# A spectral cross-attention and expert kernel: every projection from high and low parts, row sums folded twice, logits in four column groups, and a new order of the work

## The chip, the cores and the metric

The kernel runs on one core of a Trainium2 chip. The engines that matter here are TensorE (PE in the profile: matrix products; PEld is its loading of the stationary operand), VectorE (DVE), ScalarE (ACT), GpSimd (POOL) and SyncE (SP, which only issues DMAs). They run side by side and wait for each other through semaphores. The metric is the device time of one execution in microseconds (us), lower is better. The profile is of one execution of its own.

## The reference

`x` and `ctx` are 32 sequences of 512 rows of 512 numbers. Cut to what matters:

```
x = x + attention(layernorm(x), ctx)
x = x + ffn(layernorm(x))
attention: q = rows of x, scaled by a logistic map of their norm and by position
           Q, K, V = q @ Wq.T + bq, mem @ Wk.T + bk, mem @ Wv.T + bv   (mem = ctx * constant)
           QKV = hamilton(hamilton(fft(Q)*f, fft(K)*f), fft(V)*f)      (fft along the 512 rows)
           return real(ifft(QKV))
ffn:       logits = layernorm(tokens) @ gate.T; top-1 of 8 experts, capacity 4096
           out = tokens + softmax weight * (gelu(token @ wi[e]) @ wo[e])
```

## The kernel before

There are two stages. The first takes the sequences one after the other and ends with each token's row written to the slot of its expert. The second runs the eight experts over the slots. The change touches only the first.

In the first stage the Fourier transform is taken before the projection, since both are linear, and only 256 of the 512 frequencies are computed, because the signal is real. One sequence goes through these steps:

- SP loads `x_in` and `c_in`. ACT and POOL compute row statistics (`sums_x`, `squares_x`, `stats1`, the map in `logistic`, `scales1`), and ACT scales the rows in `q_of`.
- DVE folds the 512 rows to 256 sums for the even frequencies and 256 differences for the odd ones (`folds_q`, `folds_c`, two operations of 128x1024 each).
- `dft(b, w, u)` on PE: for the context (w = 0) and the query (w = 1), and for each of four blocks u of 128 columns, four f32 products with 256 moving columns against a constant matrix of cosines and sines, two for each half of a 512-column bank, `xt_ps[u % 2]`. ACT copies the bank to `c_spec` or `q_spec`.
- K and V are projected from a high and a low part of the spectrum. Both are of the type fp32r, which PE takes in one pass and rounds; high times high, low times high and high times low are added up. ACT makes `c_high` and DVE makes `c_low` (`context_low`). Q is projected by f32 products (`project(b, k, s)`; k counts Q, K and V for even and odd frequencies and s is the real or the imaginary half).
- DVE turns the spectra into complex pairs (`convert`), multiplies the quaternions (`products`, `sums`, `back_to_parts`). `inverse` on PE transforms back, and DVE adds the residual (`add_even`, `add_odd`).
- `turn` transposes the rows into `xt_ps`, `token_block` copies them to `x_tok_t`, and `logits` multiplies them by the gate: for each of four row tiles four f32 products of 8 moving columns. `choose` and `place` on DVE pick the expert and the slot. `sums_x2`, `squares_x2`, `stats2` and `base_of` compute the second layernorm's numbers and the residual row, and `store` writes it to HBM. `scatter` writes the row to its slot.

Each engine runs one hand-written list, `body(b)`, in which every call names how many sequences it lags, such as `project(b - 1, 2, 0)`. The engines take their lists strictly in order. Nothing else sets the order but the semaphores. PE's `xt_ps` has two banks, used in turn by `dft` and `turn`; `pair` has two, used in turn by the projections k, and freed by `convert`; `even_ps` and `odd_ps` serve the inverse transform, the logits and the ranks.

Of the kernel before, what the change touches and what calls it, by code (L numbers as in the profile page):

```python
# [22 lines left out]
P = 128  # L23
# [30 lines left out]
def forward_matrix():  # L54

    n = np.arange(256)[:, None]
    j = np.arange(128)[None, :]
    m = np.empty((256, 2, 2, 128))
    for tile in (0, 1):
        angle = 2 * np.pi * (((2 * j + tile) * n) % 512) / 512  # L60
        m[:, tile, 0], m[:, tile, 1] = np.cos(angle), -np.sin(angle)
    m[:, 0, 1, 0] = 1 - 2 * (np.arange(256) % 2)
    return m.reshape(2, 128, 2, 256).transpose(1, 0, 2, 3).reshape(128, -1).astype(np.float32)


def inverse_matrix():
# [6 lines left out]
    for tile in (0, 1):  # L73
        f = (2 * np.arange(128) + tile)[:, None]
        e = h[f] * np.exp(2j * np.pi * ((f * n) % 512) / 512) / 512
        m[:, tile, 0], m[:, tile, 1] = e.real, -e.imag
# [50 lines left out]
def xattn_moe_kernel(nc, x, ctx_in, wq, wk, wv, bq, bk, bv, gate, gamma, beta, wi, wo, out):  # L127
# [4 lines left out]
    c_fwd = nc.inline_tensor(forward_matrix(), "c_fwd").ap()  # L132
# [3 lines left out]
    c_tri = nc.inline_tensor(np.triu(np.ones((P, P), np.float32), 1), "c_tri").ap()  # L136
    c_eye = nc.inline_tensor(np.eye(P, dtype=np.float32), "c_eye").ap()
# [8 lines left out]
    with outer:  # L146
# [11 lines left out]
        with ExitStack() as mem:  # L158
# [6 lines left out]
            fwd = sb("fwd", [P, 2, 2, 256])  # L165
            inv = sb("inv", [P, 2, 2, 256])
            w_q = sb("w_q", [P, CB, DIM])

            w_kh, w_kl, w_vh, w_vl = (sb(n, [P, CB, DIM], f32r) for n in ("w_kh", "w_kl", "w_vh", "w_vl"))
            c_high, c_low = (sb(n, [P, CB, 512], f32r) for n in ("c_high", "c_low"))  # L170
# [7 lines left out]
            gate_g = sb("gate_g", [P, CB, EXPERTS])  # L178
# [13 lines left out]
            q_spec, c_spec = (sb(n, [P, CB, 512]) for n in ("q_spec", "c_spec"))  # L192
# [15 lines left out]
            real_row = sb("real_row", [1, 3, 2, DIM])  # L208
# [7 lines left out]
            x_tok_t = [sb(f"x_tok_t{i}", [P, CB, P]) for i in (0, 1)]  # L216
# [22 lines left out]
            SETUP_DMAS = 15  # L239
            ZEROED = len(values) + 5  # L240
# [6 lines left out]
            w_split, c_split = sem("w_split"), sem("c_split")  # L247
# [12 lines left out]
            f1_mm, f1_ev = sem("f1_mm"), sem("f1_ev")  # L260
# [5 lines left out]
            g_mm, g_ev, logit_mm = sem("g_mm"), sem("g_ev"), sem("logit_mm")  # L266
            route, exp_done, rank_mm = sem("route"), sem("exp_done"), sem("rank_mm")
# [6 lines left out]
            SETUP = 14  # L274

# [11 lines left out]
            with nc.Block() as block:  # L287

                @block.sync
                def _(sp):  # L290
# [9 lines left out]
                    def load_x(b):  # L300
                        if not on(b) or isinstance(b, int) and b < 2:
                            return
                        sp.wait_ge(qf_ready, b * 2)
                        sp.dma_start(x_in, seq(x, b)).then_inc(x_loaded, 16)

                    def load_c(b):
                        if not on(b) or isinstance(b, int) and b < 2:
                            return
                        sp.wait_ge(cf_ready, b * 2)
                        sp.dma_start(c_in, seq(ctx_in, b)).then_inc(c_loaded, 16)  # L310

                    def real_out(b):
# [3 lines left out]
                        sp.dma_start(bins_in, real_row[:].rearrange("o a s n -> o (a s n)")).then_inc(real_left, 16)  # L316
                        if last_sequence(b):
                            sp.wait_ge(qf_ready, BATCH * 2)
                            sp.wait_ge(cf_ready, BATCH * 2)
# [62 lines left out]
                    sp.dma_start(fwd[:].rearrange("p a b c -> p (a b c)"), c_fwd).then_inc(fwd_in, 16)  # L382
                    sp.dma_start(pos[:], c_pos).then_inc(pos_in, 16)
                    for dst, src in ((signs[:].rearrange("p a b c -> p (a b c)"), c_sgn),
                                     (tri32, c_tri), (eye[:], c_eye), (token[:], c_tok),
                                     (iota8[:].rearrange("p t e -> p (t e)"), c_exp),
                                     (w_q[:], wq.rearrange("(k p) n -> p k n", p=P)),
                                     (kv_raw[:, 0], wk.rearrange("(k p) n -> p k n", p=P)),
                                     (kv_raw[:, 1], wv.rearrange("(k p) n -> p k n", p=P)),
                                     (inv[:].rearrange("p a b c -> p (a b c)"), c_inv),  # L390
                                     (gate_t[:], gate.rearrange("(k p) e -> p k e", p=P)),
# [6 lines left out]
                    sp.wait_ge(cf_ready, 2)  # L398
                    sp.dma_start(c_in, seq(ctx_in, 1)).then_inc(c_loaded, 16)
                    sp.wait_ge(qf_ready, 2)  # L400
# [4 lines left out]
                    def body(b):  # L405
                        real_spread(b - 3)
                        real_gather(b - 3)
                        real_store(b - 3)
                        store(b - 4)
# [15 lines left out]
                def _(pe):  # L425
                    def dft(b, w, u):
# [6 lines left out]
                        if u == 0:  # L433
                            pe.wait_ge(ready, b * 2 + 2)
# [1060 lines left out]
```

## Time and profile before

| | |
|---|---|
| median of 3 runs | 3565.24 us (3561.56 to 3566.55) |
| the profiled execution | 3560.93 us, span on the core 3559.1 us |
| mean granted TensorE clock | 0.986 of full speed |
| PE busy | 3459.5 us (97%) |
| DVE busy | 2547.8 us (72%) |
| ACT busy | 1610.9 us (45%) |
| POOL busy | 1264.8 us (36%) |

The span is measured from the first instruction to the last. The busy shares are over both stages; the windows of the trace part them. In a line of the timeline, the first number is the start, the second how long the group took; the ends of products are modelled and overlap the next, so that the time of a product is read from one start to the next. An f32 product leaves two records, an fp32r product one.

### The profile page before, as it was taken

What the parts mean: (1) busy time and instruction counts of PE and PEld (TensorE: products, weight loads), DVE (VectorE), ACT (ScalarE), POOL (GpSimd) and SP (SyncE); (2) the same over time, 40 slices, a digit from 0 to 9 for tenths busy, and PEclk for the clock granted to TensorE, in tenths of its full rate; (3) what the DMA queues carried; (4) which work ended last, traced back from release to release, by engine and by line L of the source; (5) the groups of instructions that cost most, each with busy time, mean ns of one, the idle gap of its engine ahead of it and who ended that gap; (6) DMA issues with size and microseconds to landing.
All of it is one profiled execution on the core that took longest, in us unless ns stands there. A gap on an engine that the chain in (4) does not pass through costs nothing. (4 is left out here: it accounts for less than half of the span.)

```text
span 3559.1 us, 46918 instructions
## 1 busy us (share of the span) xinstructions
PE 3459.5 (97%) x15056; PEld 2634.4 (74%) x15056; DVE 2547.8 (72%) x3536; ACT 1610.9 (45%) x2948; POOL 1264.8 (36%) x1607
## 2 busy tenths in 40 slices
PE   7999999999999999999999959999999999999998
PEld 5766777767776777776777648888888888888886
DVE  4999999999999999989899954444444444444443
ACT  4545545455454554545545333333333333333332
POOL 2556656466565565656566530000000000000000
PEclk9999999999999999999999969999999999999999
DMA  5421221211212112121121123333333333333331
GB/s 201 153 104 59 73 83 59 81 62 59 83 48 95 60 59 95 71 83 48 59 95 60 60 81 104 109 119 118 120 119 119 117 119 106 107 105 119 107 108 41
DMA packets 223433, 326.65 MB, mean 92 GB/s; under 512 B 36880, under 2 KB 102672, under 8 KB 223280
## 3 DMA queue, kind: packets, MB, share of 16 engines
q1 hardware_dynamic: 207952, 307.97, 25.1%
q0 software_dynamic: 15360, 16.99, 1.4%
q8 instruction: 86, 1.41, 0.2%
q14 instruction: 35, 0.29, 0.0%
HBM read 256.82 MB, written 101.97 MB: 101 GB/s over the span
## 5 line engine op out<-in xcount | busy, mean ns | idle before, releaser
L1372 ACT ACTIVATE act<-hid_ps 128x512 f32<-128x512 f32 x256 | 153.1, 598 | 797.5 <-PE hid_ps L1299 797.5
L1433 DVE CAST act_h<-act 128x512 fp32r<-128x512 f32 x256 | 109.3, 427 | 523.2 <-ACT act L1372 523.2
L1253 POOL TENSOR_TENSOR tally<-tally,unit 1x1 f32<-1x1 f32 x16 | 2.9, 180 | 1350.2 <-DVE mixed L1445 1350.2
L468 PE MATMUL pair<-w_q,q_spec 128*128 128x512 f32 x1024 | 457.6, 595 | 11.6 <-DVE s L989 10.7
L1299 PE MATMUL hid_ps<-tok_h,w_h 128*128 128x512 f32 x1024 | 405.5, 396 | 0.2 <-issue 0.2
L1299 PE MATMUL hid_ps<-tok_l,w_h 128*128 128x512 f32 x1024 | 399.3, 390 | 0.0
L1299 PE MATMUL hid_ps<-tok_h,w_l 128*128 128x512 f32 x1024 | 398.7, 389 | 0.0
L1315 PE MATMUL out_ps<-w_l,act_h 128*128 128x512 f32 x1024 | 398.5, 389 | 0.0
L1314 PE MATMUL out_ps<-w_h,act_l 128*128 128x512 f32 x1024 | 398.3, 389 | 0.0
L1313 PE MATMUL out_ps<-w_h,act_h 128*128 128x512 f32 x1024 | 398.3, 389 | 0.0
L1427 DVE TENSOR_TENSOR w_l<-w_raw,w_h 128x2048 fp32r<-128x2048 f32 x128 | 293.4, 2293 | 90.9 <-ACT w_h L1366 90.9
L468 PEld LDWEIGHTS pair<-w_q,q_spec 128*128 128x128 f32 x1024 | 191.9, 190 | 220.9 <-issue 204.7
L667 ACT ACTIVATE q_spec<-xt_ps 128x512 f32<-128x512 f32 x128 | 76.5, 598 | 534.8 <-PE xt_ps L442 534.8
L442 PE MATMUL xt_ps<-fwd,c_fold 128*128 128x256 f32 x1024 | 253.4, 392 | 15.7 <-DVE c_fold L921 11.6
L1366 ACT ACTIVATE w_h<-w_raw 128x2048 fp32r<-128x2048 f32 x128 | 244.5, 1911 | 10.0 <-PEq L287 10.0
L442 PEld LDWEIGHTS xt_ps<-fwd,c_fold 128*128 128x128 f32 x1024 | 198.8, 197 | 60.1 <-issue 27.1
L442 PEld LDWEIGHTS xt_ps<-fwd,q_fold 128*128 128x128 f32 x1024 | 195.7, 191 | 55.7 <-issue 28.7
L442 PE MATMUL xt_ps<-fwd,q_fold 128*128 128x256 f32 x1024 | 232.9, 381 | 2.8 <-DVE q_fold L921 2.8
L1299 PEld LDWEIGHTS hid_ps<-tok_l,w_h 128*128 128x128 f32 x1024 | 192.3, 188 | 41.1
L1299 PEld LDWEIGHTS hid_ps<-tok_h,w_h 128*128 128x128 f32 x1024 | 192.6, 188 | 39.4 <-issue 1.6
L1314 PEld LDWEIGHTS out_ps<-w_h,act_l 128*128 128x128 f32 x1024 | 192.2, 188 | 40.0
L1313 PEld LDWEIGHTS out_ps<-w_h,act_h 128*128 128x128 f32 x1024 | 192.2, 188 | 39.9
(172 smaller groups left out, 7931.5 us busy)
## 6 DMA issues: line engine op xcount, KB each, us to landing
w_raw<-in_L_ffn_wi SPq DMA_DIRECT2D x128, 512.0 KB, 3.5
w_raw<-in_L_ffn_wo SPq DMA_DIRECT2D x128, 512.0 KB, 4.5
w_raw<-in_x SPq DMA_DIRECT2D x32, 1024.0 KB, 5.4
w_raw<-in_ctx SPq DMA_DIRECT2D x32, 1024.0 KB, 7.7
x_res<-in_x SPq DMA_DIRECT2D x31, 1024.0 KB, 9.8
out<-x_res SPq DMA_DIRECT2D x31, 1024.0 KB, 4.3
slots<-rows SPq DMA_DIRECT2D x4, 4160.0 KB, 17.3
got<-slots SPq DMA_DIRECT2D x15, 1040.0 KB, 7.6
```

Of the source, the lines that this page charges most:

```text
L442: last = nc.tensor.matmul(ps[:, eo * 256:eo * 256 + 256], folded[:, eo, t, u * P:(u + 1) * P], fwd[:, t, eo, :], start=(t == 0), stop=(t = ...
L468: last = nc.tensor.matmul(pair[k % 2][:, s, :], spec[:, c, tile * 256 + s * P:tile * 256 + (s + 1) * P], w[:, c, :], start=(c == 0 and n = ...
L667: nc.scalar.activation((c_spec, q_spec)[w][:, u, :], xt_ps[u % 2][:], ACT.Copy).then_inc(f1_ev, 1)
L1253: nc.gpsimd.tensor_tensor(tally[:], tally[:], unit[:], ALU.add).then_inc(tallied, 1)
L1299: last = nc.tensor.matmul(hid_ps[i % 2][:], a[:, c, :], b[:, c, :], start=first_, stop=last_)
L1313: nc.tensor.matmul(out_ps[t][:], ah, oh, start=(i == 0), stop=False)
L1314: nc.tensor.matmul(out_ps[t][:], al, oh, start=False, stop=False)
L1315: last = nc.tensor.matmul(out_ps[t][:], ah, ol, start=False, stop=(i == ISTEPS - 1))
L1366: nc.scalar.activation(w_h[k % RING][:], w_raw[k % 2][:], ACT.Copy).then_inc(wh_ready, 1)
L1372: nc.scalar.activation(act32[i % 2][:], hid_ps[i % 2][:], ACT.Gelu).then_inc(gelu, 1)
L1427: v.tensor_tensor(w_l[k % RING][:], w_raw[k % 2][:], w_h[k % RING][:].bitcast(f32), ALU.subtract).then_inc(wl_ready, 1)
L1433: v.tensor_copy(act_h[i % 4][:], act32[i % 2][:]).then_inc(ah_ready, 1)
```

## The change

The change has five parts, all in the first stage.

1. **Query from parts too.** `w_q` becomes `w_qh` and `w_ql`, and the query's spectrum `q_high` and `q_low`. All six projections of a sequence are then three fp32r products for each block, where Q had one f32 product.
2. **Low parts made in the bank.** ACT copies the bank of a transformed block rounded to `c_high` or `q_high` (`spectrum_high`), PE adds minus the identity times that high part to the same bank (`remove_high`, one fp32r product with 512 moving columns), and ACT copies what is left (`spectrum_low`). DVE's `context_low` and ACT's `context_high` are gone, and so are `c_spec` and `q_spec`.
3. **Rows folded twice.** The even frequencies are split once more: the 256 sums are folded again into 128 sums and 128 differences (`fold_again`), so that each half of the even frequencies takes one product of 128 moving columns.
4. **Logits in four column groups.** `gate_w` is now the stationary operand with 32 columns, and the tokens move. Each of the four blocks of the contraction writes its own 32 partitions of `even_ps`, ACT copies these partial sums (`logits_out`), and `logits_turn` adds and transposes them by four products with a constant matrix.
5. **New order** on every engine's list. Two small changes go with it: `real_row` uses three partitions, and the constant DMAs of the setup are 16 instead of 15.

The diff, cut to its core:

```diff
-                            pe.wait_ge(ready, b * 2 + 2)
+                            pe.wait_ge(ready, b * FOLD + FOLD)
...
-                        for eo in range(2):
-                            for t in range(2):
-                                last = nc.tensor.matmul(ps[:, eo * 256:eo * 256 + 256],
-                                                        folded[:, eo, t, u * P:(u + 1) * P], fwd[:, t, eo, :],
-                                                        start=(t == 0), stop=(t == 1))
+                        even = ps[:, 0:256].rearrange("p (s h j) -> p h s j", s=2, h=2)
+                        for h in range(2):
+                            nc.tensor.matmul(even[:, h], folded[:, 0, h, u * P:(u + 1) * P], fwd_e[:, h],
+                                             start=(h == 0), stop=True,
+                                            skip_group_check=True)
+                        for t in range(2):
+                            last = nc.tensor.matmul(ps[:, 256:512], folded[:, 1, t, u * P:(u + 1) * P], fwd_o[:, t],
+                                                    start=False, stop=True,
+                                            skip_group_check=True)
                         last.then_inc(f1_mm, 1)
+
+                    def remove_high(b, w, u):
...
+                        pe.wait_ge(f1_high, b * 8 + w * 4 + u + 1)
+                        nc.tensor.matmul(xt_ps[u % 2][:], minus_eye[:], (c_high, q_high)[w][:, u, :],
+                                         start=False, stop=True, skip_group_check=True).then_inc(f1_rest, 1)
...
-                        terms = ((q_spec, w_q),) if which == 0 else ((c_high, wh), (c_low, wh), (c_high, wl))
+                        high, low = (q_high, q_low) if which == 0 else (c_high, c_low)
+                        terms = ((high, wh), (low, wh), (high, wl))
...
-                            last = nc.tensor.matmul(even_ps[:, t * EXPERTS:(t + 1) * EXPERTS], x_tok_t[t % 2][:, c, :],
-                                                    gate_g[:, c, :], start=(c == 0), stop=(c == CB - 1))
+                            last = nc.tensor.matmul(even_ps[32 * c:32 * c + 32, h * 256:h * 256 + 256], gate_w[:, c, :],
+                                                    x_tok_t[:, :, c, :], start=True, stop=True, tile_position=(0, 32 * c))
...
+                        pe.wait_ge(logit_ev, b + 1)
+                        for t in range(ROWT):
+                            o = LOGITS + t * EXPERTS
+                            last = nc.tensor.matmul(odd_ps[:, o:o + EXPERTS], parts[:, t * P:(t + 1) * P], chosen[:],
+                                                    start=True, stop=True)
...
+                        nc.scalar.activation((c_high, q_high)[w][:, u, :], xt_ps[u % 2][:], ACT.Copy).then_inc(f1_high, 1)
...
+                        act.wait_ge(f1_rest, b * 8 + w * 4 + u + 1)
+                        nc.scalar.activation((c_low, q_low)[w][:, u, :], xt_ps[u % 2][:], ACT.Copy).then_inc(f1_low, 1)
...
-                        for eo, op in ((0, ALU.add), (1, ALU.subtract)):
-                            v.tensor_tensor(dst[:, eo], src[:, 0:2], src[:, 2:4], op).then_inc(ready, 1)
+                        v.tensor_tensor(dst[:, 1], src[:, 0:2], src[:, 2:4], ALU.subtract).then_inc(ready, 1)
+                        v.tensor_tensor(src[:, 0:2], src[:, 0:2], src[:, 2:4], ALU.add).then_inc(ready, 1)
+
+                    def fold_again(b, src, dst, ready):
+                        dve.wait_ge(ready, b * FOLD + 2)
+                        v.tensor_tensor(dst[:, 0, 0], src[:, 0], src[:, 1], ALU.add).then_inc(ready, 1)
+                        v.tensor_tensor(dst[:, 0, 1], src[:, 0], src[:, 1], ALU.subtract).then_inc(ready, 1)
```

PE's new list, in which one place matters below (`dft` and `remove_high` share the two banks):

```diff
+                        project(b - 2, 5, 1)
+                        dft(b - 1, 0, 1)
+                        remove_high(b - 1, 0, 0)
+                        remove_high(b - 1, 0, 1)
+                        dft(b - 1, 0, 2)
+                        dft(b - 1, 0, 3)
+                        remove_high(b - 1, 0, 2)
...
+                        logits(b - 3, 1)
                         project(b - 1, 4, 0)
+                        logits_turn(b - 3)
+                        dft(b, 0, 0)
                         project(b - 1, 4, 1)
+                        project(b - 1, 5, 0)
```

On PE, where the query's blocks are transformed between the two inverse transforms, this stood before (L442 is `dft`, L502 `inverse`; the rows named ISA or REGISTER_ALU carry waits):

```order
L442 MATMUL xt_ps<-fwd,q_fold 128x256 x4
L124 REGISTER_ALU
L442 MATMUL xt_ps<-fwd,q_fold 128x256 x4
L124 REGISTER_ALU
L442 MATMUL xt_ps<-fwd,q_fold 128x256 x4
L499 ISA
L502 MATMUL even_ps<-r_spec,inv 128x512 x2
```

And this stands on PE behind a body's start now, for the context's blocks 1 to 3 (L468 and L472 are `dft`, L483 is `remove_high`; the banks alternate):

```order
L468 MATMUL xt_ps<-fwd_e,c_fold 128x2x64 x2
L472 MATMUL xt_ps<-fwd_o,c_fold 128x256 x2
L482 ISA
L483 MATMUL xt_ps<-c_high,minus_eye 128x512
L482 REGISTER_ALU
L483 MATMUL xt_ps<-c_high,minus_eye 128x512
L468 MATMUL xt_ps<-fwd_e,c_fold 128x2x64 x2
L472 MATMUL xt_ps<-fwd_o,c_fold 128x256 x2
```

Four products have become two short ones and two long ones, and each block has a product of its own between the two copies by ACT. The second `remove_high` stands directly behind the first.

On ACT, this stood before around the residual pass (L698 is `base_of`, L667 `spectrum`, L683 `real_part`, L691 `real_bin`, L637 `decay`, L643 and L647 `logistic`, ten steps in all; the scaling of the query's rows, `q_of`, comes further down):

```order
L691 ACTIVATE real_row<-pair0 1x1024
L707 ACTIVATE x_tok_t1<-xt_ps1 128x512
L698 ACTIVATE x_res<-rows0 128x512 x4
L667 ACTIVATE c_spec<-xt_ps0 128x512
L683 ACTIVATE re1<-pair1 128x512
L691 ACTIVATE real_row<-pair1 1x1024
L637 ACTIVATE map_e<-norm1 128x4
L643 ACTIVATE map_y0<-map_s,minus_half 128x4
L647 ACTIVATE map_y1<-map_y0,centre 128x4
```

And this stands there now (L757 is `base_of`, L712 `q_of`, L727 `spectrum_high`, L733 `spectrum_low`, L742 `real_part`, L782 `exps`):

```order
L757 ACTIVATE x_res<-rows1 128x512 x4
L710 REGISTER_ALU
L712 ACTIVATE w_raw0<-w_raw0,q_bias,q_scale 128x512 x4
L138 REGISTER_ALU
L727 ACTIVATE c_high<-xt_ps0 128x512
L740 REGISTER_ALU
L138 REGISTER_ALU
L742 ACTIVATE re0<-pair0 128x512
L727 ACTIVATE c_high<-xt_ps1 128x512
L733 ACTIVATE c_low<-xt_ps0 128x512
L781 ISA
L782 ACTIVATE e_over<-over 128x32
```

The map has moved ahead of `base_of`, `q_of` stands directly behind it, and the first copies of the context's spectrum, for which `remove_high` and the next `dft` wait, stand behind both.

## Rows read from the trace of the kernel before

**Rows 1.** The page: busy time, share of the span and instructions.

```profile
PE 3459.5 (97%) x15056; PEld 2634.4 (74%) x15056; DVE 2547.8 (72%) x3536; ACT 1610.9 (45%) x2948; POOL 1264.8 (36%) x1607
```

**Rows 2.** Busy time in three stretches: loops, drain, experts.

```profile
core 0: us, PE busy (x) PEld busy (x) DVE busy (x) ACT busy (x) POOL busy (x), PEclk, DMA share, GB/s
1000.00:1500.00 500.00, 494.92 (x2127) 353.15 (x2126) 454.05 (x665) 267.57 (x589) 287.63 (x372) 1.00 0.21 74
2055.00:2111.00 56.00, 27.19 (x120) 18.89 (x120) 26.69 (x60) 18.72 (x43) 24.12 (x36) 0.59 0.17 57
2111.00:3559.00 1448.00, 1427.61 (x6400) 1179.72 (x6400) 690.84 (x832) 525.97 (x577) 67.78 (x82) 0.99 0.32 110
```

**Rows 3.** PE timeline, one body: start us, us, line, operation, count.

```profile
1000.98 0.48 PE L468 MATMUL pair<-w_vh,c_high 128*128 128x512 f32 x1
1001.29 0.40 PE L468 MATMUL pair<-w_vh,c_low 128*128 128x512 f32 x1
...
1006.52 1.89 PE L442 MATMUL xt_ps<-fwd,c_fold 128*128 128x256 f32 x8
1008.25 3.60 PE L468 MATMUL pair<-w_q,q_spec 128*128 128x512 f32 x8
...
1044.35 7.13 PE L468 MATMUL pair<-w_q,q_spec 128*128 128x512 f32 x16
1051.32 0.95 PE L527 MATMUL even_ps<-gate_g,x_tok_t 128*128 128x8 f32 x8
1052.13 0.63 PE L516 MATMUL xt_ps<-eye,rows 128*128 128x128 f32 x4
1052.60 1.91 PE L527 MATMUL even_ps<-gate_g,x_tok_t 128*128 128x8 f32 x16
```

**Rows 4.** PE timeline, fifteen bodies later: the same projection.

```profile
1994.75 7.11 PE L468 MATMUL pair<-w_q,q_spec 128*128 128x512 f32 x16 [0.56 <-DVE s L989]
```

**Rows 5.** DVE groups, 500 to 2000 us: count, busy us, mean ns, idle before.

```profile
L986 DVE TENSOR_TENSOR s<-re,pair 128x256 f32<-128x256 f32 x141 | 57.9, 411 | 13.5 <-ACT real_row L691 13.5
...
L921 DVE TENSOR_TENSOR q_fold<-w_raw 128x1024 f32<-128x1024 f32 x48 | 56.5, 1217 | 23.1 <-ACT w_raw L655 23.1
L937 DVE TENSOR_TENSOR c_low<-c_spec,c_high 128x2048 fp32r<-128x2048 f32 x24 | 54.7, 2279 | 0.0
...
L1062 DVE TENSOR_TENSOR rows<-x_res,even_ps 128x512 f32<-128x512 f32 x48 | 32.7, 682 | 40.1 <-DMA x_res<-in_x 36.0 <-PE even_ps L502 4.1
...
L1086 DVE TENSOR_TENSOR logit<-even_ps,rows 128x32 f32<-128x32 f32 x23 | 4.4, 192 | 32.7 <-PE even_ps L527 32.7
```

**Rows 6.** DVE timeline, three operations of one group of sums.

```profile
1007.48 1.22 DVE L1026 TENSOR_TENSOR prod<-prod 128x1024 f32<-128x1024 f32 x1
1008.73 0.69 DVE L1028 TENSOR_TENSOR s<-prod 128x512 f32<-128x512 f32 x1
1009.34 0.68 DVE L1029 TENSOR_TENSOR s<-prod 128x512 f32<-128x512 f32 x1
```

**Rows 7.** POOL timeline: first row of the query's scale, first and last of the second statistics.

```profile
1009.81 0.27 POOL L808 TENSOR_TENSOR st<-map_y,slope 128x4 f32<-128x4 f32 x1 [3.38 <-ACT map_y L647]
...
1048.71 2.31 POOL L825 TENSOR_TENSOR tt<-square,inv_dim 128x4 f32<-128x4 f32 x1 [4.50 <-ACT unused L606]
...
1061.63 2.25 POOL L835 TENSOR_TENSOR rows<-neg,rows 128x4 f32<-128x4 f32 x1
```

**Rows 8.** ACT timeline: copies, and the two passes that wait for POOL.

```profile
1013.84 2.93 ACT L655 ACTIVATE w_raw<-w_raw,q_bias,q_scale 128x512 f32<-128x512 f32 x4 [1.66 <-POOL q_bias L812]
...
1028.35 0.60 ACT L667 ACTIVATE q_spec<-xt_ps 128x512 f32<-128x512 f32 x1 [10.62 <-PE xt_ps L442]
...
1043.90 1.91 ACT L676 ACTIVATE c_high<-c_spec 128x2048 fp32r<-128x2048 f32 x1
...
1063.92 2.93 ACT L698 ACTIVATE x_res<-rows 128x512 f32<-128x512 f32 x4 [6.33 <-POOL rows L835]
```

**Rows 9.** PE timeline at the start.

```profile
53.84 0.80 PE L468 MATMUL pair<-w_kh,c_high 128*128 128x512 f32 x1 [3.96 <-DVE w_vl L944]
```

More of the change, by code:

```diff
@@ L274, in xattn_moe_kernel @@
             SETUP = 14
+            FOLD = 4
+            LOGITS = 64
             TILE_DONE = (3, 7, 4, 8)
@@ L549, in body @@
+                        inverse(b - 3, 1, 0)
+                        inverse(b - 3, 1, 1)
+                        turn(b - 3, 1 - p, 0)
+                        project(b - 1, 0, 0)
+                        project(b - 1, 0, 1)
+                        turn(b - 3, 1 - p, 1)
                         project(b - 1, 1, 0)
                         project(b - 1, 1, 1)
-                        dft(b, 0, 1)
-                        logits(b - 3, 3)
+                        turn(b - 3, 1 - p, 2)
+                        logits(b - 3, 0)
@@ L573, in body @@
-                        turn(b - 2, p, 1)
-                        project(b, 0, 0)
-                        project(b, 0, 1)
-                        logits(b - 2, 0)
-                        turn(b - 2, p, 2)
-                    for b in range(6):
+                        project(b - 1, 5, 0)
+                    for b in range(7):
                         body(b, b % 2)
-                    with pe.Fori(6, 30, 2) as b:
-                        body(b, 0)
-                        body(b + 1, 1)
@@ L583, in _ @@
-                    for b in range(30, BATCH + 3):
+                    with pe.Fori(7, 29, 2) as b:
+                        body(b, 1)
+                        body(b + 1, 0)
+                    for b in range(29, BATCH + 4):
                         body(b, b % 2)
@@ L749, in _ @@
+                        logits_out(b - 3)
+                        base_of(b - 3, 1 - p)
+                        q_of(b)
+                        spectrum_high(b, 0, 0)
+                        real_part(b - 1, 4)
+                        spectrum_high(b, 0, 1)
+                        spectrum_low(b, 0, 0)
+                        exps(b - 3)
+                        spectrum_low(b, 0, 1)
+                        spectrum_high(b, 0, 2)
+                    for b in range(6):
                         body(b, b % 2)
-                    with act.Fori(7, 29, 2) as b:
-                        body(b, 1)
-                        body(b + 1, 0)
@@ L753, in _ @@
-                    for b in range(29, BATCH + 4):
+                    with act.Fori(6, 30, 2) as b:
+                        body(b, 0)
+                        body(b + 1, 1)
+                    for b in range(30, BATCH + 3):
                         body(b, b % 2)
```

328 lines of the change are left out of this document (175 added, 153 removed).

## The prediction

> **What bounds the kernel now.** I read the page first: PE is busy for 97% of the span and DVE for 72% [rows 1]. These are means over two stages, and the windows part them. In the loops PE is busy for 494.9 of 500 us and DVE for 454.1; in the experts' 1448 us DVE is under one half, and the change does not touch them [rows 2]. So the change acts in the first stage, and there PE sets the pace, with DVE close behind. The timeline gives the period: the query's first projection starts at 1044.35 and, fifteen bodies later, at 1994.75, so 950.4 / 15 = 63.36 us a sequence [rows 3, 4]. PE's busy part of it is 0.990 x 63.36 = 62.7 us, and 0.6 us is waits.
>
> For DVE, the groups tell what it waits for. In the 1500 us, or 23.7 bodies, it sat idle 13.5 us for ACT's one-row copy, 23.1 for the scaled query rows, 36.0 for the residual's load and 32.7 for the logits [rows 5]: 105.3 / 23.7 = 4.4 us a body. The rest of its idle time lies inside its own chains. DVE's own work thus takes 63.4 - 4.4 = 59.0 us. This is the second floor, and only 3.7 us under PE's.
>
> **The change on PE, per sequence.** Starts are compared with starts, since the ends of products are modelled.
>
> - Query from parts. Sixteen f32 records, which are eight products of 512 columns, take 1051.32 - 1044.35 = 6.97 us. The 24 fp32r products of a V projection take 1006.52 - 1000.98 = 5.54 us for the same amount of work, so 0.23 us each [rows 3]. Two query projections: 2 x (6.97 - 5.54) = 2.9 us less.
> - Folded twice. A block's four f32 products of 256 columns take 1008.25 - 1006.52 = 1.73 us, so 0.43 us each [rows 3], as much per column as those of 512. Two of the four halve their columns. No row shows an f32 product of 128 columns. By columns it is 0.215 us. From below the loading of the weights bounds it: four products with 8 columns take 1052.13 - 1051.32 = 0.81 us, 0.20 each [rows 3], and that lies under 0.215. From above it is 0.43, no gain. I take 0.215, since it is next to the row for 8 columns, where only the loading counts: 8 x 2 x 0.215 = 3.4 us less (bounds 0 and 3.7).
> - Removing the high part. Eight fp32r products of 512 columns are added. In a row each takes 0.23 us, but the first behind an f32 product takes 1001.29 - 1000.98 = 0.31 [rows 3]: 8 x 0.31 = 2.5 us more (bounds 1.8 and 2.5).
> - Logits. The four row tiles cost 4 x 0.81 = 3.2 us. `logits_turn` is four products of 8 columns again, 0.8 us. The eight products with 256 moving columns and 32 stationary ones are not in the trace. If the four column groups run side by side, two sets cost about as much as two products of 256 columns, 2 x 0.43, with some 0.1 us each for starting, 1.1 us. If they don't, they are two sets of four such products, 2 x 1.73 = 3.5 us [rows 3]. I take the first, since the groups share neither columns nor output partitions: 3.2 - 0.8 - 1.1 = 1.3 us less (other bound: 1.1 us more).
>
> About this, "TensorEngine Tiling (Array Packing)" of the Trainium skill (Performance Considerations and Key Properties) says that four column groups bring up to four times the speed, and that a change of tiling drains the engine. "TensorE: Matmul & The Clock Gate" (Part 3) gives 2.38 times for three column groups; with that factor a set would take 1.73 / 2.38 = 0.73 us (an estimate from that page), and the sum would be 0.4 us a sequence higher. The same part says that weight loads run ahead of products in flight only where row groups differ, which here they don't; by that the groups would follow each other, which is the rival below. No row here shows column groups.
>
> Sum on PE: 62.7 - 2.9 - 3.4 + 2.5 - 1.3 = 57.6 us.
>
> **The change on DVE.** `context_low` goes: 54.7 us for 24 [rows 5], 2.2 us each by starts. Two folds get two operations of 512 columns each, which start 1009.34 - 1008.73 = 0.61 us apart, and each must see the operation before it finished, as in the sums, where the next starts 1008.73 - 1007.48 = 1.25 us after an operation of 1.22 [rows 6], some 0.1 us later than without. That is 4 x 0.61 + 2 x 0.1 = 2.6 us. DVE's floor rises by 0.4 us to 59.4 us and stands above PE's sum. What PE gives up beyond that is worth nothing.
>
> **The waits that the change adds.** ACT gets eight more copies from the bank at 0.60 us [rows 8], `logits_out` at 0.60, and loses `context_high`, 1.91 [rows 8]: 3.5 us more on an engine that is busy for 267.6 of 500 us [rows 2]. That costs nothing as work. It costs as latency, for PE now waits for ACT twice for each block. At most places another product lies between. At two it doesn't. Behind `dft(0, 1)` stand two `remove_high` and then `dft(0, 2)`, which needs ACT to have copied block 1's high part and block 0's low part: 2 x 0.60 and about 0.3 us of hand-over (an estimate), less the 0.5 us of the two products: 1.0 us. The last `remove_high` of the query waits for block 3's copy, 0.6 us. Both together 1.6 us, with everything else on PE queued behind.
>
> The same two copies stand on ACT behind `base_of` and `q_of`, which wait for POOL. There the second statistics take from 1048.71 to 1063.9, 15.2 us, and `base_of` waited 6.33 us for them [rows 7, 8]. In the new order `squares_x2` follows projection 1 on ACT. From there PE has listed, until it needs the bank for that `dft(0, 2)`, projections 2 to 5 (22.2 us), two transposes (0.9), both sets of logits and their turn (1.9), two blocks (2.6) and one `remove_high`: 28 us. The other engines have two copies, the small `decay` and the squares, some 5 us (an estimate), 15.2 for the statistics, 1013.84 - 1009.81 = 4.0 for the query's scale [rows 7, 8], 2.9 for its rows [rows 8] and 2 for the copies: 29 us. So this chain ties with PE's own work, and costs 0 to 2 us. I add 0.4.
>
> Period: 57.6 + 0.6 (the waits of now) + 1.6 + 0.4 = 60.2 us. That is 0.8 above DVE's floor of 59.4, so DVE lets it through, but only if most of its 4.4 us of waits go. They should, as three of the four end when PE or ACT behind PE delivers, and DVE now is the later one.
>
> **The sum.** The first stage has 31 periods between its first and last sequence: 31 x (63.36 - 60.2) = 98 us less. At the start K's first projection stood at 53.84, behind the low part of V's weights [rows 9]; the weights now come in the same way with one split more (2.2 us), and the folds are 0.7 us longer: 3 us more. The drain, 56 us of it with PE half idle [rows 2], goes through the same chain; I put it at nothing, give or take 10 us. The profiled execution took 3560.9 us, the median 3565.2. So 3560.9 - 98 + 3 = 3466, and 2 us more for the middle between the two: **3468 us**.
>
> **The rivals.**
>
> - *The column groups follow one another* (14%). 2.4 us a sequence dearer on PE: 62.6 us, 31 x 0.76 = 24 less, 3541 us. For it: the weights are f32 and every f32 product loads twice. Against: nothing in the rows.
> - *DVE's floor is all that counts* (13%). If PE's waits at the banks vanish behind DVE's pace: 59.4 us, 31 x 3.96 = 123 less, 3442 us.
> - *ACT and POOL pace it* (12%). If the chain above costs its 2 us, or `remove_high` waits at more places: 61.8 us, 31 x 1.56 = 48 less, 3518 us.
> - *Slower: DVE keeps its waits* (7%). DVE's floor has gone up by 0.4 us. If its 4.4 us of waits stay, because each hangs on a chain through POOL and DMA and not on PE's pace (the load of the residual alone is 36.0 us of them [rows 5], and it starts when `base_of`'s rows are stored), the period is 59.4 + 4.4 = 63.8 us, 31 x 0.4 = 14 us more with 3 for the start: 3580 us. It decides from waits of 4.0 us on.
>
> My forecast has 50%, with a range of its own from 3445 to 3500. The other 4% are a net of nothing. The range over all reaches from 3432 to 3542, which leaves out the slower case and the ends. What a measurement of this kernel can tell from no change is about 0.2%, 7 us. Faster by more than that: 88%; within it: 5%; slower: 7%.
>
> **What would show it.** Right: two Q projections starting some 60 us apart; a block's transform of 1.3 us; each set of logits 0.4 to 0.6 us; PE's share in the loops down to 96% with waits for ACT's copies before L483 and L468; DVE's share up to 96%. Wrong if f32 products of 128 columns cost as much as 256 (3.4 us a sequence back, 100 us in all), if the copies by ACT delay every block, or if DVE's groups show its waits for the residual or the query as large as before.

## The result and the profile after

The changed kernel takes **3429.7 us** (median of 4 runs, 3429.1 to 3429.9) against 3563.4 us for the kernel before in the same comparison (4 runs): a ratio of 0.9625, with a 95% interval of 0.9608 to 0.9642. That is 134 us less. The forecast of 3468 us was 97 us under the 3565 us of the kernel before, and the result lies 2.3 us below the low end of the range of 3432 to 3542. The sign and the order of size were right; the period was 1 us too long.

The page after has a span of 3427.8 us and this busy line, which answers to [rows 1]:

```profile
PE 3286.5 (96%) x15568; PEld 2597.8 (76%) x15568; DVE 2571.6 (75%) x3633; ACT 1736.4 (51%) x3206; POOL 1422.2 (41%) x1608
```

The windows, which answer to [rows 2]; the experts begin 132 us earlier now, so their stretch is taken there, and the drain is left out:

```profile
core 0: us, PE busy (x) PEld busy (x) DVE busy (x) ACT busy (x) POOL busy (x), PEclk, DMA share, GB/s
1000.00:1500.00 500.00, 485.84 (x2427) 372.13 (x2426) 493.21 (x740) 315.01 (x686) 369.41 (x404) 1.00 0.24 79
...
1979.00:3427.00 1448.00, 1427.42 (x6400) 1179.18 (x6400) 690.80 (x832) 526.00 (x577) 68.35 (x82) 0.99 0.33 110
```

The experts are the same 1427.4 us of PE in the same 1448 us, so everything happened in the first stage. There the two engines have changed places. DVE went from 454 to 493 of 500 us, and PE from 495 to 486. PE's share of the whole span, still 96%, hides this. DVE's 75% hides it more: it is a mean over loops at 98.6% and experts at 48%.

The period is read from an operation that comes once a sequence, the copy `logits_out` on ACT. The columns are count, shortest/median/longest ns, first and last start:

```profile
L776 ACT ACTIVATE x_tok_t<-even_ps x16: 597/598/601, 1004.1 to 1892.5; 128x512 f32<-128x512 f32 x16
```

So (1892.5 - 1004.1) / 15 = **59.23 us** a sequence, against 63.36 before. 31 times the difference is 128 us of the 134. DVE's list alone was put at 59.4.

Some of these 128 us are TensorE's clock, which the forecast did not look at. (PEclk in the windows is the granted clock as a share of full speed.) The kernel before in one stretch of its loops (columns as above):

```profile
611.00:613.00 2.00, 2.00 (x7) 1.55 (x6) 1.97 (x3) 1.85 (x4) 1.92 (x2) 0.50 0.00 0
```

Here the granted clock was 0.50, the lower of TensorE's two levels (1.2 GHz), with PE busy throughout. Short stretches like it lie near 228, 928, 1119 and 1689 us too. Read from one copy `c_high` to the next, the sequences from 400 to 1900 us in which one of them fell took 64.3 to 64.5 us, and the others 62.9 to 63.7. In the changed kernel the clock stayed full from 40 us to the drain (1.00 in the window above). At some 1.2 us each the five make about 6 us of the 128 (an estimate from these periods), and two of them, 0.2 us a sequence, are in the 63.36.

What each engine waited for, 500 to 1900 us, which is 23.6 sequences. First PE, with total us, times and the longest; then DVE:

```profile
PE pair L506 <- DVE s L1067: 18.4, 23, 0.8
PE xt_ps L483 <- ACT q_high L727: 11.0, 24, 0.5
PE xt_ps L483 <- ACT c_high L727: 10.4, 23, 0.5
DVE rows L1140 <- PE even_ps L540: 1.3, 1, 1.3
```

Of DVE's waits before, 105 us for the one-row copy, the query's rows, the residual and the logits [rows 5], not one is left. The rows of those two engines also give PE's account: 0.9717 x 59.23 = 57.6 us busy, 21.4 / 23.6 = 0.9 us for ACT's copies, 18.4 / 23.6 = 0.8 us for DVE. The last is the sign that DVE leads: PE finds the `pair` bank not yet read by `convert`.

DVE's groups, 500 to 2000 us, answer to [rows 5]. They are `convert`, the query's fold, and the context's fold, which is the same operation:

```profile
L1064 DVE TENSOR_TENSOR s<-re,pair 128x256 f32<-128x256 f32 x144 | 58.9, 409 | 0.0
L996 DVE TENSOR_TENSOR q_fold<-w_raw 128x1024 f32<-128x1024 f32 x23 | 32.1, 1397 | 0.0
L996 DVE TENSOR_TENSOR c_fold<-w_raw 128x1024 f32<-128x1024 f32 x23 | 28.0, 1217 | 0.0
```

The first two showed 13.5 and 23.1 us of waiting before, and the sum that takes the residual 36.0 for its load; for these causes they now show none. The query's fold takes 1397 ns, though it took 1217 before [rows 5] and the context's still does. What runs beside it is GpSimd's work on the one-row copy:

```profile
1017.77 1.58 POOL L925 TENSOR_TENSOR real_in<-real_in,bias 16x96 f32<-16x96 f32 x1
1019.04 1.41 DVE L996 TENSOR_TENSOR q_fold<-w_raw 128x1024 f32<-128x1024 f32 x1
```

In the two bodies looked at (1000 to 1119 us), two of the eight operations of 128x1024 in `sums` stand beside later GpSimd operations on the same row and take 1.60 and 1.47 us; the other six take 1.21. With the rest of the query's folds (1335 ns for 1217, 802 for 683) that is 0.2 + 0.1 + 0.1 + 0.4 + 0.3 = about 1.1 us a sequence by which DVE's list is longer beside GpSimd. In the kernel before, the same sums were 0.4 us longer than at 1.21 each (means of 1.25 and 1.28) and the folds not at all.

The terms on PE, from its timeline (start us, us, line, operation, count). First a set of logits in column groups, then a stretch of the new transforms:

```profile
1003.38 0.64 PE L565 MATMUL even_ps<-x_tok_t,gate_w 128*32 128x256 f32 x8
1003.95 0.50 PE L506 MATMUL pair<-w_kh,c_high 128*128 128x512 f32 x1
...
1018.33 0.58 PE L483 MATMUL xt_ps<-c_high,minus_eye 128*128 128x512 f32 x1
1019.37 0.50 PE L483 MATMUL xt_ps<-c_high,minus_eye 128*128 128x512 f32 x1 [0.45 <-ACT c_high L727]
1019.86 0.71 PE L468 MATMUL xt_ps<-fwd_e,c_fold 128*128 128x128 f32 x4
...
1025.22 0.61 PE L468 MATMUL xt_ps<-fwd_e,q_fold 128*128 128x128 f32 x4
1025.66 1.03 PE L472 MATMUL xt_ps<-fwd_o,q_fold 128*128 128x256 f32 x4
1026.53 0.61 PE L468 MATMUL xt_ps<-fwd_e,q_fold 128*128 128x128 f32 x4
```

A set of logits (8 records, four f32 products with 256 columns) takes 1003.95 - 1003.38 = 0.57 us, where four ordinary products of 256 columns took 1.73 [rows 3]: the four groups run side by side. A block's transform takes 1026.53 - 1025.22 = 1.31 us, of which the two products with 128 columns take 0.44. Both were forecast (0.55 and 1.3). The wait in brackets is at the first of the two places where the prediction saw PE held by ACT, behind `dft(0, 1)`; the prediction gave that place 1.0 us.

### The profile page after: what moved, and what is told of

It reads as the page before. It is cut to its first block and busy times, and to the rows that moved or that the text cites. A ratio compares the mean times of both kernels' runs of the same rounds, so it can differ in the third digit from the quotient of the medians.

```text
span 3427.8 us, 48342 instructions
## 1 busy us (share of the span) xinstructions
PE 3286.5 (96%) x15568; PEld 2597.8 (76%) x15568; DVE 2571.6 (75%) x3633; ACT 1736.4 (51%) x3206; POOL 1422.2 (41%) x1608
## 5 line engine op out<-in xcount | busy, mean ns | idle before, releaser
L742 ACT ACTIVATE re<-pair 128x512 f32<-128x512 f32 x192 | 114.4, 596 | 229.8 <-PE pair L506 229.8
L958 POOL DMA_INDIRECT slots<-rows,slot_i x128 | 210.6, 1645 | 45.6 <-issue 45.6
L506 PE MATMUL pair<-w_vh,c_high 128*128 128x512 f32 x512 | 202.9, 396 | 21.6 <-DVE s L1067 21.6
L1392 PEld LDWEIGHTS out_ps<-w_l,act_h 128*128 128x128 f32 x1024 | 192.2, 188 | 40.0
L1376 PEld LDWEIGHTS hid_ps<-tok_h,w_l 128*128 128x128 f32 x1024 | 192.5, 188 | 37.9
L506 PE MATMUL pair<-w_kh,c_high 128*128 128x512 f32 x512 | 212.6, 415 | 0.0
L506 PE MATMUL pair<-w_qh,q_high 128*128 128x512 f32 x512 | 205.5, 401 | 1.5 <-ACT q_low L733 1.5
```

What stands on the lines that cost most here:

```text
L506: last = nc.tensor.matmul(pair[k % 2][:, s, :], spec[:, c, tile * 256 + s * P:tile * 256 + (s + 1) * P], w[:, c, :], start=(c == 0 and n = ...
L742: nc.scalar.activation(re_buf[k % 2][:], pair[k % 2][:, 0, :], ACT.Copy).then_inc(re_ready, 1)
L958: nc.gpsimd.indirect_dma_start(slots, bass.IndirectOffsetOnAxis(ap=slot_i[p][:, t:t + 1].bitcast(u32), axis=0), rows[p][:, t, :], None, bo ...
L1376: last = nc.tensor.matmul(hid_ps[i % 2][:], a[:, c, :], b[:, c, :], start=first_, stop=last_)
L1392: last = nc.tensor.matmul(out_ps[t][:], ah, ol, start=False, stop=(i == ISTEPS - 1))
```

## The experiments

Every kernel below is the changed one with one edit, whose main lines are shown. DVE lighter, DVE heavier, the logits by tile and the first kernel with folding on GpSimd ran in one group, the others in a second one with the changed kernel itself beside them. The kernel before took 3570.8 us in the first group and 3562.9 us in the second (medians; its single runs go from 3561 us at a mean granted clock of 0.985 to 3577 us at 0.980), so the times below are good to some 5 us between groups; ratios are to the kernel before of the same group. The periods come from the same copy as above and don't depend on that.

### Which engine sets the pace: DVE lighter and DVE heavier

```diff
@@ sums (run e1_dve_light)
-hc.step(v.tensor_tensor(prod[:, 0], prod[:, 0], prod[:, 1], ALU.subtract))
+hc.step(v.tensor_tensor(prod[:, 0, 0], prod[:, 0, 0], prod[:, 1, 0], ALU.subtract))
@@ fold (run e2_dve_heavy)
+v.tensor_tensor(dst[:, 0], src[:, 0:2], src[:, 2:4], ALU.add).then_inc(ready, 1)
 v.tensor_tensor(dst[:, 1], src[:, 0:2], src[:, 2:4], ALU.subtract).then_inc(ready, 1)
```

> The changed kernel with VectorE's load lightened: in `sums` the first subtraction works on 512 instead of 1024 columns, so half of that difference is left out of the result. VectorE saves four times 0.53 us a sequence. Theory A (VectorE's own list is the bound, and TensorE's own pace with its waits for ScalarE's copies is below it, 57.6 us busy + 0.9 at L483 + some 0.1 = 58.6 us): the period falls from 59.25 to 58.6 us, 31 x 0.65 = 20 us less, about 3410 us. Theory B (the prediction's, TensorE's waits for the copies add up to a pace of its own of 59.3 us or more, and VectorE is only level with it): no change, 3428 to 3431 us.

> The changed kernel with one more VectorE operation of 128x1024 in each of the two folds (the sums are written once more), 1.14 us each by starts. Theory A (VectorE is the bound without slack): all of it shows, 32 x 2.28 = 73 us more, about 3503 us. Theory B (TensorE's waits for ScalarE set the pace and VectorE has slack at the fold): clearly less than 60 us more.

Lighter: **3404.4 us**, 0.9531 (0.9515 to 0.9547). Heavier: **3507.4 us**, 0.9819 (0.9802 to 0.9835). The window in the loops of the lighter kernel (columns as above):

```profile
1000.00:1500.00 500.00, 491.78 (x2444) 376.19 (x2443) 482.42 (x746) 317.20 (x694) 347.51 (x396) 1.00 0.24 80
```

its waits on PE (the one for `c_high` is alike, 10.4 us) and DVE:

```profile
PE xt_ps L483 <- ACT q_high L727: 10.6, 23, 0.5
DVE s L1064 <- ACT real_row L750: 26.4, 16, 2.5
```

and its copy `logits_out`:

```profile
L776 ACT ACTIVATE x_tok_t<-even_ps x15: 586/597/600, 1051.4 to 1867.7; 128x512 f32<-128x512 f32 x15
```

Of the heavier, the same three views:

```profile
1000.00:1500.00 500.00, 471.83 (x2326) 359.76 (x2325) 492.65 (x720) 302.80 (x661) 330.40 (x384) 0.99 0.22 74
```

```profile
PE pair L506 <- DVE s L1068: 54.6, 23, 2.6
```

```profile
L776 ACT ACTIVATE x_tok_t<-even_ps x14: 597/598/600, 1045.1 to 1849.9; 128x512 f32<-128x512 f32 x14
```

The heavier one has a period of 804.8 / 13 = 61.9 us, 2.7 more than the changed kernel, and two operations of 1.22 and some 1.35 us were added: DVE had no slack at all. Theory A of that run holds (about 3503 us). PE's wait for `convert` grew from 0.8 to 2.4 us a sequence; besides, it waits 0.3 us for the residual's sum, and its busy part grew from 57.6 to 58.4 us with the granted clock at 0.99 on average where it was 1.00. The lighter one takes 2.1 us from DVE and gains only 0.9: 816.3 / 14 = 58.3 us. There PE's waits for DVE are gone (but for the last sequences, behind 1850 us), DVE waits for ACT's copy behind PE (26.4 us), and PE's account is full: 0.9836 x 58.3 = 57.3 busy and 0.9 for ACT's copies. So 58.3 us is **PE's own pace**, waits included, where the prediction had 60.2. DVE stands 0.9 us above it. Theory A holds here too, 6 us too high with its 3410 us, and theory B (no change) is out.

### The parts of the change, each undone alone

```diff
@@ logits by tile again, gate as moving operand (run e3_logits_old)
-    last = nc.tensor.matmul(even_ps[32 * c:32 * c + 32, h * 256:h * 256 + 256], gate_w[:, c, :],
-                            x_tok_t[:, :, c, :], start=True, stop=True, tile_position=(0, 32 * c))
+    last = nc.tensor.matmul(even_ps[:, t * EXPERTS:(t + 1) * EXPERTS], x_tok_t[:, t % 2, c, :],
+                            gate_g[:, c, :], start=(c == 0), stop=(c == CB - 1))
@@ body of PE and of ACT
-    logits_turn(b - 3)
-    logits_out(b - 3)
@@ folded once (run e4_fold_once)
-    nc.tensor.matmul(even[:, h], folded[:, 0, h, u * P:(u + 1) * P], fwd_e[:, h],
+    nc.tensor.matmul(ps[:, 0:256], folded[:, 0, h, u * P:(u + 1) * P], fwd_o[:, h],
@@ folds_q and folds_c
-    fold_again(b, q_rows, q_fold, qf_ready)
-    fold_again(b, c_in, c_fold, cf_ready)
@@ Q by float32 products (run e5_query_f32)
-    terms = ((high, wh), (low, wh), (high, wl))
+    terms = ((q_high, w_qh),) if which == 0 else ((c_high, wh), (c_low, wh), (c_high, wl))
@@ remove_high and spectrum_low
-    if not on(b):
+    if not on(b) or w == 1:
         return
```

> The changed kernel with part 4 undone: logits as sixteen f32 products of 8 moving columns per sequence, no partial sums, one copy by ScalarE less. TensorE's work grows by 3.2 - 0.8 - 1.1 = 1.3 us. Theory A (TensorE's own pace is 58.6 us, hidden under VectorE's 59.25): the pace becomes 59.9, 31 x 0.65 = 20 us more, about 3450 us. Theory B (TensorE's own pace is already 59.3 us): 31 x 1.3 = 40 us more, about 3470 us.

> The second folding is undone: the rows are folded once, and the even frequencies take two products of 256 columns again (they are taken against the matrix of the odd frequencies, so the output's even frequencies are wrong; the work is that of the kernel before). VectorE loses 2.8 us of each sequence (two sums of 128x512 for Q and two for the context), TensorE gains 3.4 us by the forecast's sum. Theory A (a sequence takes the larger of VectorE's list, 59.25 us, and TensorE's own pace, 58.25 us as the run with the lighter VectorE showed): TensorE's pace becomes 61.6 to 61.9, 31 times 2.5 more, 3505 to 3515 us. Rival B (VectorE's list alone sets the time): it is 2.8 us shorter, so the kernel is faster, at 3400 us.

> Q's projection is made by float32 products again, and nothing is subtracted in the bank for Q (its low part isn't made); everything else as changed. TensorE gains 2.9 us of products and loses four subtracting products, half of 2.5 us: +1.65; ScalarE loses four copies; VectorE's list is as it was. Theory A (the larger of the two lists): 58.25 + 1.65 = 59.9 us a sequence, 0.65 above VectorE's, 20 us more than the changed kernel, 3450 us. Rival B (TensorE's work is covered by VectorE's list even here): 3430 us. Rival C (the copies that TensorE waits for are what holds it, and they are gone for Q): TensorE 0.5 us better than by A, 3435 us.

> The changed kernel itself, once more, to stand beside the three other kernels of this group on one chip. Expected 3430 us, 0.9625 of the kernel before. If it is off by more than 0.3% of that, the comparisons of the other kernels go by this run and not by the first one.

The changed kernel again: 3429.3 us, 0.9621 (0.9605 to 0.9637), as in the first comparison.

| undone | us | ratio (95%) | period us | PE busy us of it | us above the changed |
|---|---|---|---|---|---|
| column groups | 3441.7 | 0.9638 (0.9622 to 0.9654) | 59.6 | 58.7 | 12 (between groups) |
| second folding | 3510.6 | 0.9850 (0.9834 to 0.9867) | 61.7 | 60.8 | 81 |
| Q from parts | 3438.6 | 0.9648 (0.9632 to 0.9664) | 59.5 | 59.1 | 9 |

The kernel without column groups: the window, and two of its logits' products 14 sequences apart (834.3 / 14 = 59.6):

```profile
1000.00:1500.00 500.00, 492.49 (x2469) 391.69 (x2468) 491.41 (x731) 309.20 (x674) 369.49 (x399) 1.00 0.24 78
```

```profile
1009.46 1.85 PE L566 MATMUL even_ps<-gate_w,x_tok_t 128*128 128x8 f32 x16
...
1843.74 1.85 PE L566 MATMUL even_ps<-gate_w,x_tok_t 128*128 128x8 f32 x16
```

The kernel folded once: the window, DVE's waits, and the copy that gives the period:

```profile
1000.00:1500.00 500.00, 492.19 (x2317) 376.86 (x2316) 448.45 (x673) 303.45 (x664) 303.26 (x388) 1.00 0.21 69
```

```profile
DVE rows L1137 <- PE even_ps L539: 65.6, 23, 2.9
DVE cand L1180 <- PE odd_ps L585: 59.1, 23, 2.7
```

```profile
L775 ACT ACTIVATE x_tok_t<-even_ps x16: 597/598/601, 924.1 to 1849.8; 128x512 f32<-128x512 f32 x16
```

The kernel with Q by float32 products, the window and the copy (PE's only wait, for `c_high`, is 10.4 us in 1400):

```profile
1000.00:1500.00 500.00, 496.37 (x2237) 340.55 (x2235) 492.74 (x731) 295.34 (x650) 356.68 (x400) 1.00 0.24 78
```

```profile
L776 ACT ACTIVATE x_tok_t<-even_ps x15: 598/598/601, 1009.7 to 1842.8; 128x512 f32<-128x512 f32 x15
```

- *Second folding.* VectorE has 2.8 us less to do and the kernel is 81 us slower: PE's pace is 61.7, DVE waits 124.7 us for it in 1400. Rival B is out. Theory A forecast 3505 to 3515. 61.7 - 58.3 = 3.4 us is what the second folding takes from PE, the forecast's number. The changed kernel gets 2.5 of them, down to DVE's list.
- *Column groups.* 59.6 - 58.3 = 1.3 us on PE, the forecast's number too. Only 0.4 of them show as time, since DVE hides the other 0.9: 12 us and not 40. Theory B of that run fails, and theory A, right in kind, gave 20 us with a PE pace of 59.9.
- *Q from parts.* 59.5 us. PE is the bound (99.3% busy, and its wait for Q's copy is gone with the copy), yet it is 0.4 us under the 59.9 of theory A: C, in which that wait holds PE for 0.5 us, says 3435 and comes nearest to the 3438.6; A said 3450 and B 3430.

### DVE relieved by GpSimd

The experiments say that the first 0.9 us less on DVE is worth 25 to 29 us (3429 - 3404, or 31 x 0.93). The context's second folding (two operations, 1.35 us) can go to GpSimd, which is busy for 74% of the loops.

```diff
@@ folds_c on DVE, body of POOL (run e6_pool_fold)
-fold_again(b, c_in, c_fold, cf_ready)
+pool.wait_ge(cf_ready, b * FOLD + 2)
+tv(c_fold[:, 0, 0], c_in[:, 0], c_in[:, 1], ALU.add).then_inc(cf_ready, 1)
+tv(c_fold[:, 0, 1], c_in[:, 0], c_in[:, 1], ALU.subtract).then_inc(cf_ready, 1)
@@ body of DVE, besides (run e7_pool_fold_moved)
 add_even(b - 3, 1 - p, 1)
-back_to_parts(b - 2, 0)
 add_odd(b - 3, 1 - p, 1)
+back_to_parts(b - 2, 0)
```

> The changed kernel with the context's second fold (two operations of 128x512) done by GpSimd behind `mean1` instead of VectorE. VectorE's list is 1.3 us shorter. Theory A: the period falls to TensorE's own pace of 58.6 us, 20 us less, about 3410 us, if GpSimd's work costs nothing else. Rival C (the two engines slow each other, as where GpSimd's operations of four columns take 2.1 us beside VectorE's long ones, and the query's statistics behind the fold come late): no gain or slower, 3430 to 3480 us.

> As in the run with the context's second folding on GpSimd, and VectorE now takes the sums of the odd rows, which read a PSUM bank, ahead of the parts (back_to_parts), which read and write SBUF alone. In that run two sums of SBUF operands that stood beside GpSimd's folding took 1024 and 965 ns where they take 696 and 412 ns without it, while the sums with a PSUM operand beside the same folding kept their 680 ns. Theory A (only operations on SBUF alone are held up): GpSimd's 3.1 us now lie beside four sums with a PSUM operand (2.7 us), VectorE's list is 59.25 - 1.35 + at most 0.5 = 57.9 to 58.4 us, under TensorE's pace of 58.25 to 58.6: 3400 to 3412 us, better than the changed kernel. Rival B (GpSimd slows any VectorE operation, or the parts that come later are waited for by TensorE): 3430 to 3445 us.

The first took **3443.6 us**, 0.9642 (0.9626 to 0.9658). Its period is 59.7, and not 59.2: slower than the changed kernel, with less on DVE. DVE is as full as before, so its operations must have become longer. The groups of the parts, of the changed kernel and then of this one:

```profile
L1119 DVE TENSOR_TENSOR r_spec<-s 128x512 f32<-128x512 f32 x48 | 33.4, 696 | 0.0
L1120 DVE TENSOR_TENSOR r_spec<-s 128x256 f32<-128x256 f32 x48 | 19.8, 412 | 0.0
```

```profile
L1125 DVE TENSOR_TENSOR r_spec<-s 128x512 f32<-128x512 f32 x47 | 48.1, 1024 | 0.0
L1126 DVE TENSOR_TENSOR r_spec<-s 128x256 f32<-128x256 f32 x47 | 45.3, 965 | 0.0
```

The timelines of GpSimd, then of DVE, in this kernel at that place:

```profile
1044.56 1.30 POOL L969 TENSOR_TENSOR c_fold<-w_raw 128x512 f32<-128x512 f32 x1
1045.83 1.77 POOL L970 TENSOR_TENSOR c_fold<-w_raw 128x512 f32<-128x512 f32 x1
```

```profile
1044.41 0.68 DVE L1147 TENSOR_TENSOR rows<-x_res,even_ps 128x512 f32<-128x512 f32 x1
1045.01 1.41 DVE L1125 TENSOR_TENSOR r_spec<-s 128x512 f32<-128x512 f32 x1
1046.34 1.54 DVE L1126 TENSOR_TENSOR r_spec<-s 128x256 f32<-128x256 f32 x1
```

Beside GpSimd's folding, a DVE sum that takes one operand from a PSUM bank (L1147) keeps its 0.68 us. A sum with both operands in SBUF takes 1.41 us where it takes 0.69 alone, and GpSimd's second operation is stretched as well, 1.77 for 1.30. Twice a sequence on average 0.33 + 0.55 us are 1.8 us lost for 1.35 saved.

The ends look as if the two took turns, operation by operation, and did not share a rate: GpSimd's first ends at 1045.86, and a DVE sum of 0.69 us from there would end at 1046.55 (it ends at 1046.42); GpSimd's second, 1.30 us from there, at 1047.72 (1047.60); DVE's next, 0.41 us from there, at 1048.01 (1047.88). Each is met within 0.13 us.

The second kernel puts four PSUM sums there: **3419.8 us**, 0.9594 (0.9578 to 0.9610). The changed kernel of the same group stood at 3429.3, and no run of either strays from its median by over 0.7 us, so it is 9.6 us faster; none that does the whole work is faster. Its DVE, its GpSimd, and its copy `logits_out`:

```profile
1032.47 0.69 DVE L1156 TENSOR_TENSOR rows<-rows,odd_ps 128x512 f32<-128x512 f32 x1
1033.07 0.68 DVE L1157 TENSOR_TENSOR rows<-rows,odd_ps 128x512 f32<-128x512 f32 x1
1033.67 1.31 DVE L1125 TENSOR_TENSOR r_spec<-s 128x512 f32<-128x512 f32 x1
```

```profile
1031.85 1.32 POOL L969 TENSOR_TENSOR c_fold<-w_raw 128x512 f32<-128x512 f32 x1
1033.12 1.31 POOL L970 TENSOR_TENSOR c_fold<-w_raw 128x512 f32<-128x512 f32 x1
```

```profile
L776 ACT ACTIVATE x_tok_t<-even_ps x15: 597/598/598, 1057.4 to 1880.6; 128x512 f32<-128x512 f32 x15
```

The two PSUM sums (and the one at 1031.76 ahead of them) keep 0.68 us, GpSimd's two take 1.3 each, and only the one SBUF sum that still meets GpSimd is doubled. Rival B fails, but the 3400 to 3412 us of theory A are missed: the period is 823.2 / 14 = 58.8. The doubled sum costs 0.6 a sequence, so DVE's list should be 59.2 - 1.35 + 0.6 = 58.5. The move itself costs most of the last 0.3 us, since an operation that must see the one before it finished starts some 0.1 us later [rows 6]. `add_odd`'s first sum now stands directly behind `add_even`'s second and starts 1032.47 - 1031.76 = 0.71 us after it, where the next two starts are 0.60 apart. In the same way `products` now starts 0.45 us after the last part, where `add_odd` started 0.34 us after it. Over 20 sequences the two make 0.24 us a sequence, and no other step of DVE's list grew. So DVE's list still sets the pace at 58.8, with waits of 1.6 us in 1400; PE, at 58.3, waits 7.8 us for `convert`.

The Trainium skill says of this pair, in "GPSIMD Engine Reference" (section Specifications), that GpSimd's SBUF interfaces are shared with VectorE, with contention for VectorE instructions that have two SBUF inputs. The two traces agree, 1.41 against 0.69 us with two SBUF inputs and 0.68 with one.

## Why the forecast was off, step by step

**The terms of work were right.** The transforms by 128 columns gave 3.4 us (forecast 3.4, by undoing them), the column groups 1.3 (1.3), Q from parts less its removing products 1.2 by the pace, and 1.65 with the 0.45 us of waiting that goes when Q's copies go (forecast 2.9 - 1.25 = 1.65), and PE's busy time came out at 57.6 (57.6). DVE's list is 59.2 (59.4), but that is luck in part: GpSimd stretches it by about 0.7 us more than before, which the forecast did not have, and the 59.0 us it started from held idle time inside DVE's chains that has shrunk (DVE was busy for 57.6 of its 59.0 us then, for 58.4 of 59.2 now). The rival in which the column groups follow one another is out, at 0.57 us a set. The Trainium skill's rule in "TensorE: Matmul & The Clock Gate" (Part 3), by which loads run ahead only where row groups differ, does not hold the four column groups back in this trace (0.57 us); the 0.73 us a set that the prediction worked out from its figure for three groups was too long.

**The step that failed is "57.6 + 0.6 (the waits of now) + 1.6 + 0.4 = 60.2 us. That is 0.8 above DVE's floor".** PE's own pace is 58.3, as the lighter DVE shows. So the ranking was wrong way round: DVE is the bound, as in the rival "DVE's floor is all that counts". That rival had 13% and gave 3442 us; its period of 59.4 is 0.2 above the measured one. The 1.9 us too many are made of four:

- *0.6 us, the waits of now.* The waits of PE in the kernel before, 500 to 2000 us, should have been looked up one by one:

```profile
PE pair L468 <- DVE s L989: 7.5, 19, 0.8
PE even_ps L502 <- DVE rows L1063: 6.0, 15, 0.8
```

  13.5 / 23.7 = 0.57 us: all of them are waits for DVE. They say nothing of PE's own pace; where DVE's floor stands beside PE's sum as a second bound, they are counted twice.
- *0.7 us, two ways of counting.* The two waits behind ACT's copies are there, at the places named. By starts, `dft(0, 2)` begins 1019.86 - 1018.33 = 1.53 us after the first `remove_high`, 0.99 later than two such products take (forecast 1.0); at the query's last `remove_high` the same difference is 0.8 (forecast 0.6). But the row shows [0.45]. The rest lies in the 0.58 us of the record before it, whose end is modelled, so it is part of the busy share already. Busy time from shares, and waits from differences of starts, can't be added. By the rows of waits the two places cost 21.4 / 23.6 = 0.9 us, and not 1.6, on top of a busy sum.
- *0.2 us, PE's busy time.* The forecast's 62.7 us is taken from a window with one of the half-clock stretches in it, some 0.2 us a sequence that the changed kernel doesn't have. The lighter kernel, where PE waits for nothing but ACT, is busy for 57.3 us, 0.2 to 0.3 below the forecast's 57.6; that the clock is the whole of this is argued and not shown.
- *0.4 us, the chain through POOL.* It costs nothing. The second statistics run from 1056.25 to 1063.0 now, 6.8 us and not 15.2 [rows 7]. The rows of POOL's statistics after, and ACT's first copy of the context's blocks in the body before:

```profile
1056.25 0.19 POOL L901 TENSOR_TENSOR tt<-square,inv_dim 128x4 f32<-128x4 f32 x1
1062.65 0.39 POOL L911 TENSOR_TENSOR rows<-neg,rows 128x4 f32<-128x4 f32 x1
```

```profile
1017.41 0.60 ACT L727 ACTIVATE c_high<-xt_ps 128x512 fp32r<-128x512 f32 x1 [5.57 <-issue]
```

  ACT is through with `q_of` at 1011.85 and idle for 5.6 us then. The block has been in its bank since 1008.8; by the code the copy waits until PE's last V projection, which ends at 1017.2, has read the old `c_high`. So this copy hangs on PE and not on the chain, which had been priced with durations that belonged to the old neighbours on DVE.

**DVE's waits.** That "most of its 4.4 us of waits go" held fully: 1.6 us in 1400 are left. The slower rival fell there.

**The start** was put at +3 us and is -2: K's first projection stands at 51.84 (53.84 in [rows 9]) and waits for nothing. One split more was counted, but not that `context_low` no longer stands ahead of the splits on DVE, which I argue and did not test. The drain gave no more than a microsecond or two.

Together: 31 x (60.2 - 59.23) = 30 us, the start 5, the 2 us added for the middle of the runs, and about 1 unexplained make the 38 us between 3468 and 3429.7.

## What to carry to other kernels

Give each engine a pace of its own before ranking them, and leave out of it every wait for the other candidate; where two paces lie within a microsecond or two, the answer is the larger one, not the one with margins added. Don't add waits read from starts to work read from busy shares. Look up the granted clock of the window that a busy time is taken from. When an engine has just become the bound, the next gain is to take work from it, and where GpSimd takes it, put DVE operations with a PSUM operand beside it. The changed kernel itself still has about 1.1 us a sequence of such meetings on DVE, which no run here has moved.

## What was unexpected of the hardware

- Four float32 products on four column groups, 256 columns each, took 0.57 us together, 3.0 times faster than four ordinary ones (1.73 us).
- A 128x512 sum on DVE with both operands in SBUF doubled from 0.69 to 1.41 us beside one on GpSimd; with one operand in PSUM it stayed at 0.68.
- GpSimd's eleven small operations of the second statistics took 15.2 us in the kernel before and 6.8 here, the same list on 128x4 elements. What DVE ran beside them had changed: then, four of the eleven took 2.1 to 2.3 us each and ended within 0.1 us of a DVE operation of 128x2048 whose operands are all in SBUF, as the one at 1048.71 [rows 7] did with

```profile
1048.69 2.28 DVE L1012 TENSOR_TENSOR prod<-s,s 128x2048 f32<-128x2048 f32 x1
```

  Now none of them runs beside such an operation, and the first takes 0.19 us. That this is the reason is read from the rows; no run moves only this.
